# From float32r to scaled fp16 pairs in the dense stages of a recurrent kernel, with power-of-two scales found on the way

## The chip, the cores and the metric

The kernel runs on one core of a Trainium2 chip. Its engines are TensorE (PE, matrix products into PSUM), VectorE (DVE), ScalarE (ACT), GpSimd (POOL) and SyncE (SP, which issues the DMAs); each follows its own list of instructions in order and they meet through semaphores. The metric is the device time in microseconds of one execution.

## What is computed

Two layers with residuals, for 16 sequences of 512 steps with 512 features. The first is a two-layer block with a low-rank term made from a condition vector; the second is a recurrence.

```python
c = layernorm(cond) * gamma + beta
w = gelu(c @ W1 + bias1) @ W2 + bias2           # 512 x 16384, split into a1, b1, a2, b2 of 512 x 8 per sequence
u = einsum('btd,bdr->btr', x, a2)
mid = gelu(x @ base_down + einsum('btr,blr->btl', u, b2))
v = einsum('blr,btl->btr', b1, mid)
x = 2 * x + mid @ base_up.T + einsum('bkr,btr->btk', a1, v)
xW = x @ Wx + b
h[t] = tanh(xW[:, t] + h[t - 1] @ Wh)           # 512 steps, one after the other
return x + h
```

## The kernel before

**Layout.** Features lie on the partitions (KT = 4 tiles of 128), columns are 16 sequences times 32 steps, COLS = 512. The 512 steps of the recurrence are cut into 16 chunks of 32.

**The recurrence** (`chunk`, all engines). A step n has 32 products of 128x128 weights with 32 columns in fp16 (L1091: the state as a high and a low half, `hs`, times two parts of Wh) in two halves f = 0, 1 of the output features. `place` (L596, L599) on ScalarE has put x W of the step beside them in the same PSUM tile. VectorE sums the parts (L925, `z`), ScalarE takes tanh (L679, `hf`), VectorE splits the result into `hs` (L930 high, L933 low) and TensorE starts the next step. GpSimd adds h to x1 (L556), once a step; tanh of a step waits for the addition three steps back, since `hf` has four buffers.

**The dense stages.** While the recurrence works on chunk c, chunk c + 1 goes through its stages, and c + 2 through the first of them. The order is a table of slots: slot r of chunk n is run in step r of scan chunk n - 1, a negative slot in step r + 32 of scan chunk n - 2. `dense_slot(n, r)` stands in every engine's list and is called once a step behind the recurrence's part. The stages are `mid` (slots -1 to 9), `out` (11 to 21) and `xw` (21 to 29), of 48 products each, 128x128 weights with 512 columns (L1075): every operand is held as a float32r high part and its residual, and three passes are made, high x high, high x low, low x high. The rank terms add 16 products of 256 columns to `mid` and `out` (L1078), and `rank_in` (L1064) makes u in slot -2 and v in slot 10. Around them, for each of four tiles: VectorE transposes x (L830, `xt`), ScalarE rounds it to the high part (L616, `xhi`), VectorE takes the residual (L839, `xlo`); ScalarE computes gelu twice from PSUM, in full and rounded (L639, L640, slots 4, 5, 7, 9), VectorE the residual (L865, `mlo`); VectorE makes x1 (L869, slots 15, 17, 18, 21), ScalarE and VectorE split it (L645, L874); ScalarE evacuates x W (L652, `xwev`). VectorE also transposes finished output back (L888, `turn_y`). For u and v VectorE selects the diagonal blocks (L845), rounds them (L848) and takes the residual (L852); ScalarE copies the parts in place (L625, L632).

**Ahead of the recurrence** lies a load phase of `STREAM` = 40 half steps, in which W2 streams in (L476), the factors a1, b1, a2, b2 are made, the weights are split and chunk 0 goes through its dense stages. In the last chunk, where there is no dense work, TensorE gets three filler products a step (L1237, fp16, 128x128 weights with 512 columns of `wh_s`, into a PSUM bank that nobody reads).

The kernel's own order for two of the engines, in a step:

```python
for f in range(2): place(n + 1, f)              # ScalarE, behind tanh of both halves
if c + 1 < NC: dense_slot(c + 1, t)
if c + 2 < NC: dense_slot(c + 2, t - TC)
```

## Time and profile before

| what | value |
|---|---|
| median of 3 runs | 1217.7 us (1214.39 to 1218.43) |
| the profiled execution, its own time | 1219.28 us |
| its span, first to last instruction | 1217.2 us |
| mean granted TensorE clock | 0.987 of full |
| load phase, to the first step of the recurrence | some 134 us |
| a chunk of 32 steps with dense work | 67.9 us |
| the last chunk, without | some 57 us |

Busy time is the share in which an engine had an instruction under way; of TensorE it says little, since products overlap. The chain of work that ended last is the view that tells which engine sets the end. A row of the chain in order of time has its start, its length and its number of instructions; a row of the timeline has start, length, engine, line, operation, output and inputs, and in brackets how long the engine had been idle before it and who ended that.

### The profile page before, as it was taken

How to read it: one execution, taken by the hardware profiler on the slowest of the kernel's cores; microseconds unless marked ns; L12 is line 12 of the kernel's file. 1: busy time of each engine (PE TensorE's matmuls, PEld its weight loads, DVE VectorE, ACT ScalarE, POOL GpSimd, SP SyncE). 2: the span in 40 equal slices, each digit the busy share in tenths (PEclk: the TensorE clock that was granted, in tenths of full speed). 3: DMA queues.
4: the chain of work that ended last, by engine and by line, in shares of the span. 5: the costliest groups of instructions: out<-in, count | busy, mean ns of one | idle time of the engine just before them, and what ended most of it. 6: DMA issues, size and time to landing. Idle time of an engine off the chain costs nothing.

```text
span 1217.2 us, 50835 instructions
## 1 busy us (share of the span) xinstructions
PE 1189.4 (98%) x21046; PEld 959.8 (79%) x21046; DVE 893.3 (73%) x3648; ACT 640.5 (53%) x2648; POOL 254.6 (21%) x523
## 2 busy tenths in 40 slices
PE   8977999999999999999999999999999999999998
PEld 7544888888888888888888888888888888888755
DVE  4433577887877787887877777878778777877676
ACT  4121455656555655656555655656555556555443
POOL 0000122222222222222222222222222222222221
PEclk8888999999999999999999999999999999999999
DMA  9899211312221221312221221212121211102021
GB/s 316 314 397 324 36 20 21 54 21 37 36 36 23 37 38 20 55 20 41 34 37 23 38 34 29 46 20 49 26 38 31 35 29 31 27 3 37 2 46 28
DMA packets 260565, 75.73 MB, mean 62 GB/s; under 512 B 247952, under 2 KB 248096, under 8 KB 260336
## 3 DMA queue, kind: packets, MB, share of 16 engines
q1 hardware_dynamic: 258112, 72.35, 25.2%
q8 instruction: 166, 2.72, 1.1%
q14 instruction: 63, 0.52, 0.2%
q10 hardware_dynamic: 2224, 0.14, 0.2%
HBM read 55.68 MB, written 16.78 MB: 60 GB/s over the span
## 4 chain that ended last, share of the span: by engine, by line
PE 92%; DMA 4%; ACT 1%; DVE 1%; issue 1%; SPq 0%; POOLq 0%; POOL 0%
PE bulk L1075 47%; PE rec L1091 34%; PE bulk L1078 5%; DMA work<-in_L_cond_W_dram 4%; PE bulk L1064 2%; PE bulk L1053 2%; ACT rec L599 1%; DVE z L925 1%; PE rec L978 0%; PE bulk L1237 0%; PE bulk L1204 0%; SPq L486 0%; PE rec L1075 0%; PE bulk L1019 0%; ACT gel L639 0%
## 5 line engine op out<-in xcount | busy, mean ns | idle before, releaser
L1091 PEld LDWEIGHTS rec<-hs,wh_s 128*128 128x128 f16 x16352 | 443.4, 96 | 134.1 <-DVE hs L933 124.0
L1091 PE MATMUL rec<-hs,wh_s 128*128 128x32 f16 x16352 | 492.8, 177 | 6.2 <-ACT rec L599 6.2
L679 ACT ACTIVATE hf<-z 128x32 f32<-128x32 f32 x1024 | 232.6, 230 | 435.5 <-DVE z L925 399.4
L556 POOL TENSOR_TENSOR work<-work,hf 128x64 f32<-128x64 f32 x512 | 253.2, 495 | 957.8 <-DVE hs L933 956.8
L925 DVE TENSOR_REDUCE z<-rec 128x32 f32<-128x96 f32 x1022 | 262.8, 257 | 190.6 <-PE rec L1091 165.4
L1075 PE MATMUL bulk<-mid_s,up_s 128*128 128x512 f32 x768 | 222.9, 410 | 0.6 <-ACT mid_s L640 0.5
L933 DVE SCALAR_TENSOR_TENSOR hs<-hf,hs 128x32 f16<-128x32 f32 x1022 | 196.6, 192 | 35.2
L1075 PE MATMUL bulk<-act_x,down_s 128*128 128x512 f32 x768 | 219.9, 410 | 0.0
L1075 PE MATMUL bulk<-act_s,wx_s 128*128 128x512 f32 x756 | 208.4, 408 | 0.0
L930 DVE TENSOR_SCALAR hs<-hf 128x32 f16<-128x32 f32 x1022 | 181.4, 178 | 6.3 <-ACT hf L679 4.9
L599 ACT ACTIVATE rec<-work 128x32 f32<-128x32 f32 x1022 | 184.9, 213 | 0.0
L1075 PEld LDWEIGHTS bulk<-mid_s,up_s 128*128 128x128 f32 x768 | 132.6, 189 | 21.2 <-ACT mid_s L640 1.5
L1075 PEld LDWEIGHTS bulk<-act_x,down_s 128*128 128x128 f32 x768 | 132.2, 189 | 21.1 <-issue 3.3
L1075 PEld LDWEIGHTS bulk<-act_s,wx_s 128*128 128x128 f32 x756 | 132.2, 189 | 21.0 <-issue 0.6
L652 ACT ACTIVATE work<-bulk,bs,scl 128x512 f32<-128x512 f32 x62 | 48.2, 777 | 26.8 <-PE bulk L1075 26.8
L869 DVE SCALAR_TENSOR_TENSOR work<-work,bulk 128x512 f32<-128x512 f32 x64 | 43.7, 683 | 14.1 <-PE bulk L1078 14.1
L1053 PE MATMUL bulk<-work,h_rep 128*32 128x256 f32 x512 | 39.4, 432 | 14.5 <-DMA work<-in_L_cond_W_dram 12.9
L1078 PE MATMUL bulk<-rank_s,b_s 128*128 128x256 f32 x256 | 49.2, 298 | 0.0
L865 DVE TENSOR_TENSOR mid_s<-gel,mid_s 128x512 fp32r<-128x512 f32 x64 | 43.7, 684 | 4.7 <-ACT mid_s L640 4.7
L625 ACT CAST rank_s<-rank_p 32x128 fp32r<-32x128 f32 x128 | 37.4, 292 | 16.5 <-DVE rank_p L848 15.4
L874 DVE TENSOR_TENSOR act_s<-work,act_s 128x512 fp32r<-128x512 f32 x64 | 43.8, 686 | 1.1 <-ACT act_s L645 0.9
L1078 PEld LDWEIGHTS bulk<-rank_s,b_s 128*128 128x128 f32 x256 | 40.2, 192 | 5.1 <-issue 1.6
(129 smaller groups left out, 681.2 us busy)
## 6 DMA issues: line engine op xcount, KB each, us to landing
work<-in_L_cond_W_dram SPq DMA_DIRECT2D x33, 1024.0 KB, 8.1
out_dram<-work SPq DMA_DIRECT2D x240, 64.0 KB, 2.5
work<-in_x_dram SPq DMA_DIRECT2D x224, 64.0 KB, 3.9
work<-in_x_dram SPq DMA_DIRECT2D x8, 256.0 KB, 9.7
work<-in_L_cond_base_up_dram SPq DMA_DIRECT2D x1, 1024.0 KB, 8.1
work<-in_L_cond_base_down_dram SPq DMA_DIRECT2D x1, 1024.0 KB, 12.9
wh_f<-in_L_cond_Wh_dram SPq DMA_DIRECT2D x1, 1024.0 KB, 16.5
wh_f<-in_L_cond_Wx_dram SPq DMA_DIRECT2D x1, 1024.0 KB, 5.4
```

Source lines behind the costliest of these rows:

```text
L556: nc.gpsimd.tensor_tensor(to, xs, hf[:, t % 4], ALU.add).then_inc(sum_done, 1)
L599: nc.scalar.activation(R[f][:, :, PARTS, :], xw[:, c % 2].rearrange("p k (b t) -> p k b t", t=TC)[:, f * HT:(f + 1) * HT, :, t], ACT.Copy) ...
L652: nc.scalar.activation(xw[:, n % 2, m], bank(at["xw_banks"][m]), ACT.Identity, bias=bs[:, m:m + 1], scale=fwd).then_inc(xw_done, 1)
L679: nc.scalar.activation(hf[:, t % 4, half], z[:, half], ACT.Tanh, scale=inv_reg).then_inc(tanh_done, 1)
L874: nc.vector.tensor_tensor(act_s[:, LO, m], x1[n % 3][:, m], act_s[:, HI, m].bitcast(F32), ALU.subtract).then_inc(x1lo_done, 1)
L925: nc.vector.tensor_reduce(z[:, half], R[f].rearrange("p m j b -> p m b j"), AX.X, ALU.add).then_inc(z_done, 1)
L930: nc.vector.tensor_scalar(hs[:, half, 0, :], hf[:, t % 4, half], H_SCALE, None, ALU.mult).then_inc(hi_done, 1)
L933: nc.vector.scalar_tensor_tensor(out=hs[:, half, 1, :], in0=hf[:, t % 4, half], scalar=H_SCALE, in1=hs[:, half, 0, :], op0=ALU.mult, op1=A ...
L1053: last = nc.tensor.matmul(bulk[j * SQ:(j + 1) * SQ, BANK_ROW + n % 2, 0:WCOLS], h_rep[:, half * HK + k].rearrange("p g e b -> p (g e b)"), ...
L1075: mm = nc.tensor.matmul(bank(banks[m]), w_s[:, w, k, m * P:(m + 1) * P], src[:, a, k, :], start=(i in starts), stop=(i in ends), skip_grou ...
L1078: mm = nc.tensor.matmul(bank(banks[m])[:, k * GC:(k + 1) * GC], rank_f[:, -1 - p, k, m * P:(m + 1) * P], rank_s[:, k * GC:(k + 1) * GC], s ...
L1091: last = nc.tensor.matmul(R[fo][:, m, 0:PARTS, :], wh_s[:, q, k, n * P:(n + 1) * P], hs[:, k, :, :], start=(m == k == q == 0), stop=(k == ...
```

## The change

Chunks 0 to 2 keep their dense stages. From chunk `F16_FROM` = 3 on, so in the scan chunks 2 to 14:

- The operands of the three dense stages are pairs of fp16 (high part and residual) in place of float32r pairs, still three passes. The rank products (L1078) and `rank_in` stay as they are.
- fp16 has a narrow range, so each operand is scaled by a power of two. The scale follows from a bound: for x, the absolute sums of the columns of a partition (ScalarE, `accum_out`); for gelu, the bound of x, the sum of u and the largest weights; for x1, the absolute sums of gelu and v. A bound per partition becomes the largest over all partitions in this way: GpSimd writes the column times the unit matrix (`diagonal`, 128x128), TensorE multiplies it with a matrix of ones (`cross`, in steps 18, 1 and 13), VectorE reduces the result from PSUM and masks out the exponent (steps 20, 3 and 15), GpSimd forms the scales from it with one-column operations, each waiting for the one ahead.
- Gelu is computed once from PSUM, with a scale; the fp16 high part is a scaled copy of it (`ghi`, slots 5, 6, 8, 9), with the residuals a step later than before.
- x1's doubling, so far part of L869, is done by GpSimd: eight additions of 128x256 in steps 24 to 31 (`DOUBLE_AT`), since x1 is now scaled out of PSUM in the same VectorE operation.
- x is transposed a good part of a chunk earlier (steps 1, 2, 13, 14); x1 gets a fourth buffer.
- The weights are turned into scaled fp16 pairs on the way: seven maxima on VectorE (`top_of`, six in the load phase, one in step 1), exchanged between partitions by a write to HBM and a broadcast read; scales in step 14; then in steps 42 to 79 36 scaled copies on ScalarE and 24 additions and subtractions of 128x512 on GpSimd (`convert`).
- `place` writes both halves of x W in one ScalarE operation of 64 columns in every step of the kernel.

```diff
+F16_FROM = 3
+XT16_AT, XT16_FIRST = (-31, -30, -19, -18), (-21, -20, -19, -18)
+XSUM_AT, XSUM_FIRST = (-30, -29, -18, -17), (-19, -18, -17, -16)
+XTOP_AT, XSCALE_AT = -16, -12
+UTOP_AT, USCALE_AT = -1, 3
+GTOP_AT, GSCALE_AT = 11, 15
+GHI_AT, MLO_AT = (5, 6, 8, 9), (6, 7, 9, 10)
+W_SCALE_AT = 14
+CROSS_AT = (XTOP_AT + 2, UTOP_AT + 2, GTOP_AT + 2)
+DOUBLE_AT = 24
+TOPS_AT = (11, 13, 23, 12, 28, 20)
+CONVERT_AT = (F16_FROM - 2) * 32 + 10
...
+            sp.dma_start(w_tops.rearrange("(q j) -> q j", j=7), wtop[:]).then_inc(w_out, 16)
+            sp.wait_ge(w_out, 16)
+            sp.dma_start(w_all[:], w_tops.rearrange("(o n) -> o n", o=1).broadcast_to([P, P * 7])).then_inc(w_back, 16)
...
+            def diagonal(n, e, column):
+
+                i = 3 * (n - F16_FROM) + e
+                if i > 0:
+                    pool.wait_ge(crossed, i)
+                nc.gpsimd.tensor_tensor(diag[:], ident[:], spread(column, P), ALU.mult).then_inc(diag_set, 1)
...
+            def state_top(n):
+
+
+                pool.wait_ge(gsum_done, (KT + 1) * (n - F16_FROM + 1))
+                link(nc.gpsimd.tensor_tensor(gr[:, 0:2], gsum[:, 0:2], gsum[:, 2:4], ALU.add))
+                link(nc.gpsimd.tensor_tensor(gr[:, 0:1], gr[:, 0:1], gr[:, 1:2], ALU.add))
+                link(nc.gpsimd.tensor_tensor(gr[:, 0:1], gr[:, 0:1], kb[:, 1:2], ALU.mult))
+                link(nc.gpsimd.tensor_tensor(gr[:, 1:2], gsum[:, 4:5], kb[:, 3:4], ALU.mult))
+                link(nc.gpsimd.tensor_tensor(gr[:, 0:1], gr[:, 0:1], gr[:, 1:2], ALU.add))
+                link(nc.gpsimd.tensor_tensor(gr[:, 0:1], gr[:, 0:1], x_most[:, n % 2, 1:2], ALU.add))
+                diagonal(n, 2, gr[:, 0:1])
...
+                j = r - DOUBLE_AT
+                if 0 <= j < 2 * KT:
+                    if j == 0:
+                        pool.wait_ge(x1lo_done, (n + 1) * KT)
+                    part = x1[n % 4][:, j // 2, j % 2 * (COLS // 2):(j % 2 + 1) * (COLS // 2)]
+                    nc.gpsimd.tensor_tensor(part, part, part, ALU.add).then_inc(doubled, 1)
...
-                nc.scalar.activation(R[f][:, :, PARTS, :],
-                                     xw[:, c % 2].rearrange("p k (b t) -> p k b t", t=TC)[:, f * HT:(f + 1) * HT, :, t],
+                nc.scalar.activation(RX, xw[:, c % 2].rearrange("p (f m) (b t) -> p f m b t", f=2, t=TC)[:, :, :, :, t],
                                      ACT.Copy).then_inc(xw_placed, 1)
...
+                    if n >= F16_FROM:
+                        nc.scalar.activation(gel[:, m], bulk[:, at["mid_banks"][m], :], ACT.Gelu,
+                                             scale=scale_of(n, I_MID)).then_inc(gel_f, 1)
+                        continue
                     nc.scalar.activation(gel[:, m], bulk[:, at["mid_banks"][m], :], ACT.Gelu).then_inc(gel_f, 1)
                     nc.scalar.activation(mid_s[:, HI, m], bulk[:, at["mid_banks"][m], :], ACT.Gelu).then_inc(gel_done, 1)
+                for m in tile_at(at["ghi"], r):
+                    act.wait_ge(gel_f, n * KT + m + 1)
+                    act.wait_ge(uscale_done, n - F16_FROM + 1)
+                    nc.scalar.activation(g16[:, HI, m], gel[:, m], ACT.Copy, scale=scale_of(n, S_G)).then_inc(gel_done, 1)
...
+                if n >= F16_FROM and r == GSCALE_AT:
+                    dve.wait_ge(crossed, 3 * (n - F16_FROM) + 3)
+                    link(nc.vector.tensor_reduce(gr[:, 1:2], bank(BANK_U)[:, 0:P], AX.X, ALU.max))
+                    power(gr[:, 2:3], gr[:, 1:2]).then_inc(g_powered, 1)
...
+            def cross(n, e):
+
+
+                pe.wait_ge(diag_set, 3 * (n - F16_FROM) + e + 1)
+                pe.wait_ge(rank_sel, 2 * n + e)
+                if e == 0 and n > F16_FROM:
+                    pe.wait_ge(g_powered, n - F16_FROM)
+                nc.tensor.matmul(bank(BANK_U)[:, 0:P], ones[:], diag[:], start=True, stop=True,
+                                 skip_group_check=True).then_inc(crossed, 1)
...
-                    dense(out, i, at["out_banks"], up_s, mid_s, a1_s, out_mm)
+                    dense(out, i, at["out_banks"], *((up_s, mid_s) if n < F16_FROM else (up16, g16)), a1_s, out_mm)
```

Three places in the engines' lists. ScalarE, steps 9, 10 and 11 of scan chunk 6; `gel` and `mid_s` are gelu in full and rounded. Before:

```order
L679 ACTIVATE hf<-z 128x32 x2
L599 ACTIVATE rec<-work 128x2x16 x2
L639 ACTIVATE gel<-bulk 128x512
L640 ACTIVATE mid_s<-bulk 128x512
L679 ACTIVATE hf<-z 128x32 x2
L599 ACTIVATE rec<-work 128x2x16 x2
```

and of the change, where `g16_51` is the fp16 pair, `cs` holds the scales, `gsum` the absolute sums and `rank` is v:

```order
L991 ACTIVATE hf<-z 128x32 x2
L861 ACTIVATE rec<-work 128x2x2x16
L924 ACTIVATE gel<-bulk,cs 128x512
L932 ACTIVATE g16_51<-gel,cs 128x512
L991 ACTIVATE hf<-z 128x32 x2
L861 ACTIVATE rec<-work 128x2x2x16
L889 ACTIVATE g_junk,gsum<-gel 128x512
L991 ACTIVATE hf<-z 128x32 x2
L861 ACTIVATE rec<-work 128x2x2x16
L889 ACTIVATE g_junk,gsum<-gel 128x512
L894 ACTIVATE rank_p<-rank,cs 128x128
L900 ACTIVATE g_junk,gsum<-rank 128x128
```

Step 9 keeps two large operations, the second now a copy of the first one's output; steps 10 and 11, which had none, get one and three.

TensorE, steps 10 to 13, before (v, then recurrence and dense `out` in turn):

```order
L1064 MATMUL bulk<-gel,b1_f 32x128 x16
L1091 MATMUL rec<-hs,wh_s 128x32 x32
L1075 MATMUL bulk<-mid_s,up_s 128x512 x5
L1091 MATMUL rec<-hs,wh_s 128x32 x32
L1075 MATMUL bulk<-mid_s,up_s 128x512 x6
L1091 MATMUL rec<-hs,wh_s 128x32 x32
L1075 MATMUL bulk<-mid_s,up_s 128x512 x5
```

and of the change:

```order
L1441 MATMUL bulk<-gel,b1_f 32x128 x16
L1468 MATMUL rec<-hs,wh_s 128x32 x32
L1452 MATMUL bulk<-g16_51,up16_52 128x512 x5
L1468 MATMUL rec<-hs,wh_s 128x32 x32
L1452 MATMUL bulk<-g16_51,up16_52 128x512 x6
L1468 MATMUL rec<-hs,wh_s 128x32 x32
L1480 MATMUL bulk<-diag,ones 128x128
L1452 MATMUL bulk<-g16_51,up16_52 128x512 x5
```

The dense products stay in their steps; the crossing comes in ahead of the five of step 13.

GpSimd, from step 11 of a scan chunk. Before, its whole list in the recurrence is one row; the rows ahead of it set up the unit matrix and a mask:

```order
L533 AFFINE_SELECT ident<-ident 128x128
L539 AFFINE_SELECT mask_b<-mask_b 128x8
L542 AFFINE_SELECT mask_b<-mask_b 128x8
L539 AFFINE_SELECT mask_b<-mask_b 128x8
L542 AFFINE_SELECT mask_b<-mask_b 128x8
L556 TENSOR_TENSOR work<-work,hf 128x64 x512
```

and of the change, steps 20 to 26 (`xr` and `cs` are the bound of x and the scales, L809 is the addition of h, L795 the doubling of x1):

```order
L809 TENSOR_TENSOR work<-work,hf 128x64 x4
L671 TENSOR_TENSOR xr<-turn_bits,xr 128x1
L719 TENSOR_TENSOR cs<-k_inv,xr 128x2
L720 TENSOR_TENSOR x_most<-xr,kb 128x1
L721 TENSOR_SCALAR x_most<-xr 128x1
L722 TENSOR_TENSOR cs<-k_pow,xr 128x1
L809 TENSOR_TENSOR work<-work,hf 128x64 x4
L795 TENSOR_TENSOR work<-work 128x256
L809 TENSOR_TENSOR work<-work,hf 128x64
L795 TENSOR_TENSOR work<-work 128x256
```

One addition a step becomes the addition plus short lists of one-column operations, and one large operation in each of the steps 24 to 31.

## Rows read from the trace of the kernel before

**Rows 1.** The page: busy time of each engine.

```profile
PE 1189.4 (98%) x21046; PEld 959.8 (79%) x21046; DVE 893.3 (73%) x3648; ACT 640.5 (53%) x2648; POOL 254.6 (21%) x523
```

**Rows 2.** The page: chain that ended last, by engine.

```profile
PE 92%; DMA 4%; ACT 1%; DVE 1%; issue 1%; SPq 0%; POOLq 0%; POOL 0%
```

**Rows 3.** Busy us of PE, PEld, DVE, ACT, POOL, clock, DMA: scan chunk 8 and last.

```profile
681.90:749.80 67.90, 67.90 (x1271) 56.30 (x1268) 53.40 (x223) 39.08 (x164) 16.15 (x32) 1.00 0.21 34
...
1156.80:1213.90 57.10, 52.36 (x1114) 34.37 (x1110) 41.91 (x208) 22.72 (x126) 11.37 (x32) 1.00 0.18 35
```

**Rows 4.** The chain in order of time, last chunk: start, length, engine, line, count.

```profile
1173.34 0.65 PE bulk L1237 x3
```

**Rows 5.** The same view, scan chunk 8 of the kernel.

```profile
706.95 1.46 PE bulk L1075 x6
708.41 0.81 PE rec L1091 x32
709.22 1.25 PE bulk L1075 x5
...
739.38 1.48 PE bulk L1075 x6
```

**Rows 6.** The same view, load phase: ones times the weight scale.

```profile
50.73 0.32 PE bulk L1191 x2
```

**Rows 7.** The timeline, TensorE, load phase: 16 fp32 products in two passes.

```profile
9.97 3.75 PE L993 MATMUL bulk<-cT,work 128*128 128x16 f32 x32
```

**Rows 8.** The timeline, ScalarE, steps 9 and 10 of scan chunk 8.

```profile
702.10 0.60 ACT L639 ACTIVATE gel<-bulk 128x512 f32<-128x512 f32 x1 [0.47 <-PE bulk L1078]
702.60 0.59 ACT L640 ACTIVATE mid_s<-bulk 128x512 fp32r<-128x512 f32 x1
703.07 0.35 ACT L679 ACTIVATE hf<-z 128x32 f32<-128x32 f32 x2
```

**Rows 9.** Groups by line and form: busy us, mean ns, idle before.

```profile
L652 ACT ACTIVATE work<-bulk,bs,scl 128x512 f32<-128x512 f32 x62 | 48.2, 777 | 26.8 <-PE bulk L1075 26.8
...
L760 DVE TENSOR_REDUCE wmax<-wh_f 128x1 f32<-128x2048 f32 x1 | 2.3, 2278 | 0.0
```

**Rows 10.** The timeline, VectorE, behind step 11 of scan chunk 8.

```profile
705.77 0.30 DVE L845 COPY_PREDICATED rank<-mask,bulk 128x128 f32<-128x128 uint32 x1
```

**Rows 11.** The timeline, GpSimd, at the kernel's start.

```profile
1.28 0.29 POOL L533 TENSOR_SCALAR_AFFINE_SELECT ident<-ident 128x128 f32<-128x128 f32 x1 [0.23 <-POOL mask_b L531]
1.53 0.19 POOL L539 TENSOR_SCALAR_AFFINE_SELECT mask_b<-mask_b 128x8 f32<-128x8 f32 x1
1.79 0.19 POOL L542 TENSOR_SCALAR_AFFINE_SELECT mask_b<-mask_b 128x8 f32<-128x8 f32 x1
```

**Rows 12.** The timeline, all engines, scan chunk 8: two additions of h.

```profile
701.90 0.36 POOL L556 TENSOR_TENSOR work<-work,hf 128x64 f32<-128x64 f32 x1 [1.30 <-DVE hs L933]
...
703.98 0.68 DVE L865 TENSOR_TENSOR mid_s<-gel,mid_s 128x512 fp32r<-128x512 f32 x1
704.14 0.74 POOL L556 TENSOR_TENSOR work<-work,hf 128x64 f32<-128x64 f32 x1 [1.88 <-DVE hs L933]
```

**Rows 13.** The same, chunk 0, where two residuals follow each other.

```profile
180.93 0.19 DVE L933 SCALAR_TENSOR_TENSOR hs<-hf,hs 128x32 f16<-128x32 f32 x1
...
181.25 0.19 DVE L933 SCALAR_TENSOR_TENSOR hs<-hf,hs 128x32 f16<-128x32 f32 x1
181.36 1.45 DVE L874 TENSOR_TENSOR act_s<-work,act_s 128x512 fp32r<-128x512 f32 x2
181.52 0.74 POOL L556 TENSOR_TENSOR work<-work,hf 128x64 f32<-128x64 f32 x1 [1.93 <-DVE hs L933]
```

**Rows 14.** The timeline, SyncE's issues, start of the recurrence.

```profile
136.43 59.71 SPq L481 DMA_DIRECT2D work<-in_x_dram  x32
```

**Rows 15.** The timeline, all engines, one step of the last chunk.

```profile
1177.01 0.35 ACT L599 ACTIVATE rec<-work 128x32 f32<-128x32 f32 x2
...
1177.33 0.88 PEld L1091 LDWEIGHTS rec<-hs,wh_s 128*128 128x128 f16 x32 [0.63 <-DVE hs L933]
```

More of the change, by code:

```diff
@@ L556, in _ @@
                     nc.gpsimd.tensor_tensor(to, xs, hf[:, t % 4], ALU.add).then_inc(sum_done, 1)
+                    if n == W_SCALE_AT:
+                        weight_scales()
+                    for j in range(24):
+                        if n == CONVERT_AT + 3 + j // 2 * 3 + j % 2:
+                            convert(j)
+                    if c + 1 < NC:
+                        other(c + 1, t)
+                    if c + 2 < NC:
+                        other(c + 2, t - TC)
         @block.scalar
@@ L679, in chunk @@
                         nc.scalar.activation(hf[:, t % 4, half], z[:, half], ACT.Tanh, scale=inv_reg).then_inc(tanh_done, 1)
-                    for f in range(2) if n + 1 < T else ():
-                        place(n + 1, f)
+                    if n + 1 < T:
+                        place(n + 1)
                     if c + 1 < NC:
@@ L911, in _ @@
                     split_weight(1, wx_f, wx_s)
+                for j in tile_at(TOPS_AT, i):
+                    top_of(j)
                 dense_slot(0, i)
```

349 lines of the change are left out of this document (313 added, 36 removed).

## The prediction

> **What bounds the kernel now.** I read the page's busy shares first: TensorE is busy 98% of the span, VectorE 73%, ScalarE 53%, GpSimd 21% [rows 1]. A busy share of TensorE alone proves little, so next comes the chain that ended last: 92% of it is TensorE, 47% the 512-column dense products of L1075, 34% the small products of the recurrence (L1091) [rows 2]. The busy time by stretch then gives the clockwork: a chunk of 32 steps takes 67.9 us and PE is busy for all 67.9 of it, at the full clock; the last chunk, which has no dense work, takes 57.1 us [rows 3]. So with dense work a step takes 67.9 / 32 = 2.12 us and TensorE is the bound; without it a step takes 57.1 / 32 = 1.78 us and the round trip TensorE, VectorE, ScalarE, VectorE, TensorE is the bound. That is the floor: per chunk no more than 67.9 - 57 = 11 us can be won, whatever becomes of TensorE.
>
> **The dense products.** In the chain of scan chunk 8 a step is 0.81 us of recurrence (32 products) and then 1.25 us for five or 1.46 to 1.48 us for six dense products [rows 5]. The difference, 0.23 us, is one product; five are 1.15, so the first of a step costs about 0.09 more. The change turns both operands into fp16. The trace has that very form, though for filler work: L1237, 128x512 in fp16, three in 0.65 us [rows 4], 0.217 us each with nothing extra for the first. So a step with five goes from 1.25 to 1.08, one with six from 1.47 to 1.30: 0.165 us saved. It is no halving: the old products already run at nearly the speed of the new. In a chunk 25 of the 30 steps with dense work begin with such a product; three begin with a rank product and two with the new crossing, and save only 5 x 0.015 = 0.07 us. Sum: 25 x 0.165 + 5 x 0.07 = **-4.4 us a chunk**. Both are TensorE time on the path, as long as the round trip of 1.78 stays below 0.81 + 1.08 = 1.89.
>
> **What TensorE gains in work.** Three products of `ones` with the diagonal per chunk, in fp32. The nearest row is L1191, also `ones` in fp32: 0.32 us in the chain, in two passes, at three columns [rows 6]. Lower bound: the 32 passes of L993, 3.75 us for 16 products, 0.23 us each [rows 7]; upper bound 0.45, since 128 columns stream through. I take L1191's: 3 x 0.32 = **+0.95**.
>
> **What the other engines do to the round trip.** (a) Step 9. Now gelu is computed twice from PSUM, 0.60 and 0.59 us, one 0.50 us behind the other, and tanh of step 10 follows at 703.07, 0.97 after the first began [rows 8]. After the change the scaled gelu must be complete before `ghi` may read it. An operand that is a pointer adds 0.09 us (L652 with two takes 777 ns [rows 9], gelu with none 0.59 [rows 8]), so 0.68, a wake (0.08 where `hs` ends at 181.44 and L556 starts at 181.52 [rows 13]; I take 0.04), then 0.68 less the overlap of 0.1: tanh starts 1.30 after, 0.33 later than now, and the path runs through it: **+0.35**. (b) Step 13. The third bound is written by GpSimd in step 11: copy_predicated ends at 706.07 [rows 10], then two ScalarE operations to about 706.7, then six linked one-column operations on GpSimd at 0.26 us (L539 to L542, which waits for it: 1.53 to 1.79) and a diagonal of 128 columns, 0.3 to 0.5 [rows 11]. That is 708.7 to 709.0, while TensorE would come to the crossing at 709.22 in the old trace [rows 5], about 0.35 earlier in the new. TensorE, with five dense products queued behind it, waits between nothing and 0.6: **+0.25**. The other two crossings have shorter lists (two and three links) and should be in time. (c) Steps 3, 15 and 20: a reduction of the crossing from PSUM (0.26 to 0.30 us) and a linked mask (0.15) on VectorE beside a large operation of 0.68. The floor of 1.78 becomes about 2.3 against TensorE's 2.0 to 2.15: **+0.35** together, 0 to 0.9. (d) GpSimd and VectorE get in each other's way. The addition L556 takes 0.36 us alone and 0.74 when VectorE's L865, with two inputs from SBUF, is under way [rows 12]; and in the other direction a second L874 that meets a waiting L556 makes two of them last 1.45 us where 0.60 + 0.68 would do [rows 13]. GpSimd now doubles x1 in eight 128x256 operations in steps 24 to 31. From L556, 0.2 fixed and 0.16 for 64 columns, such an operation takes 0.84 us. The addition starts 0.27 after the second `hs` of a step (181.25 to 181.52 [rows 13]); 0.36 or, behind a residual, 0.74 of addition and 0.84 of doubling end 1.47 to 1.85 after it, and VectorE's first `hs` of the next step, 0.32 ahead of the second, wants the same port at 1.89 - 0.32 = 1.57. Four of the eight steps have such a residual: **+0.2**, 0 to 1.4.
>
> The Trainium skill, page SBUF — State Buffer, section Who interferes with whom, says the same lock of VectorE operations with two SBUF inputs and GpSimd operations is exclusive and blocks the loser fully; the trace agrees in both directions. Its page GPSIMD Engine Reference, section Performance versus the Vector engine, gives 4497 ns for a two-input operation of 2048 elements; by that an estimate for 256 columns is 0.74 us and for 512 columns 1.3 us, and the sum would come out some 3 us lower.
>
> What costs nothing: copying the rank parts on ScalarE instead of VectorE, four absolute sums of x and four of gelu, 0.6 us each, one or two a step: ScalarE is busy 39.1 of 67.9 us [rows 3] and has 1.3 us of a step between `place` and the next tanh. If that cover were gone (an accumulating operation twice as long), steps 8 and 11 would lose about 0.2 each. x is loaded a chunk earlier; SP issues 32 loads in the first 60 us of the recurrence [rows 14], and is idle most of the time. The x transposes move to steps 1, 2, 13 and 14, where VectorE has room.
>
> **x W in one operation.** Two that take 0.35 us together become one of 64 columns, surely shorter. In the last chunk they end at 1177.36, but TensorE's weight load starts at 1177.33 for `hs` [rows 15]. So at most 0.03 us a step where the round trip binds: -0.5 us for the last chunk, nothing elsewhere.
>
> **Sum.** -4.4 + 0.95 + 0.35 + 0.25 + 0.35 + 0.2 = -2.3 us a chunk, times the 13 scan chunks (2 to 14) that run an fp16 dense chunk: **-30**. Once: twelve weight tiles are converted in steps 42 to 79, 36 scaled copies on ScalarE and 24 GpSimd operations of 128x512, each 0.2 + 512 x 0.0025 = 1.5 us. Such a one ends 0.27 + 0.36 + 1.5 = 2.1 us after the previous `hs` or later, past the moment (1.57 to 1.8) the next wants the port, and a step of chunk 1 has some 0.3 us of slack; with 0.25 us a piece, **+6** (bounds 2 and 25). Seven maxima of the weights on VectorE, 2.28 us for 2048 columns [rows 9]: six lie in the load phase, where waits of 3 to 6 us for DMA stand between VectorE's operations, +1; the seventh and the reduction over 896 columns (1 us and three links) lie in chunk 0, +1.5. The maxima travel out to HBM and back behind the loads of chunk 2, the first half of the 32 from 136.43 on, which half a microsecond apiece would bring to about 145 to 150 us [rows 14]; they are wanted at step 14, about 134 + 14 x 2.2 = 165 us, so that wait is covered. Total: -30 + 6 + 2.5 - 0.5 = -22; I take **-24**, since (b), (c) and (d) are counted as if nothing of them fell into steps of six products, which have 0.33 us of slack. The profiled execution took 1219.3 us, 1217.2 of it span, and is 1.6 above the median of the three runs; 1219.3 - 24 = 1195.3, and on the runs' scale **1194 us**.
>
> **Rivals.** *All of TensorE's gain arrives* (10%): ScalarE and VectorE delays vanish in the steps' slack; -4.4 + 0.95 = -3.45 x 13 = -45, with +4 once: 1177. For it speaks that a five-product step keeps 0.12 us above the floor; against it step 10, which already shows ScalarE's delay. *Little arrives* (16%): the diagonal is late at all three crossings and the reductions count in full, 1.2 to 2 us a chunk more: 1206 to 1220. *Slower: GpSimd's large operations hold the port* (13%). The trace has one size of this addition; if its 0.36 us grew with the columns, 256 would cost 1.43 and 512 2.9 us. Then each of steps 24 to 31 finds `hs` blocked for some 0.5 us, 4 us a chunk, 50 in all, and the conversion, 2 x 2.9 + 3 x 0.5 = 7.3 us in three steps of 6.2, falls behind, +25: about 1260. It decides from 1.1 us for 128x256, where eight delays of 0.3 eat the 2.3 of a chunk. Against it: operations on GpSimd of 8 and 128 columns take 0.19 and 0.29 us [rows 11], far from proportional. *The change is not doing what it says* is excluded: the fp16 operands stand in the new order.
>
> **Chances.** Forecast 61%, for 1183 to 1206. A measurement of this kernel tells 0.3% (3.7 us) from no change, so faster means below 1214: 0.61 + 0.10 + 10 of the 16 = 0.81; same 0.06; slower 0.13. The range of 8 in 10: 1176, the first rival, up to 1218, which leaves out most of the third.
>
> **What would show it.** Chunks of 65.5 us in place of 67.9; five dense products in 1.08 us; a chunk 1 and 2 longer than the rest by 2 to 4 us; step 10 at 2.3 us; a last chunk of 56.5 to 57. Wrong if the 128x256 operation is over 1.1 us, if TensorE waits over 0.6 us for `diag`, or if the first fp16 product of a step still costs 0.09 more: then 25 x 13 x 0.09 = 29 us are gone, and with them the gain.

## The result, and the profile after

| | before | changed |
|---|---|---|
| median, us | 1217.8 (4 runs, 1214.4 to 1218.4) | 1184.2 (4 runs, 1181.1 to 1190.6) |
| ratio | 1 | 0.9736 (0.9687 to 0.9786) |
| profiled execution, us (span) | 1219.3 (1217.2) | 1190.6 (1188.9) |
| first reduction of the recurrence at | 135.7 | 137.1 |
| from there to the end | 1081.5 | 1051.8 |

The change makes the kernel 2.6% faster, 34 us by the medians. A second comparison of the same two kernels gave 1185.5 (5 runs) against 1217.6 (9 runs), 0.9732 (0.9707 to 0.9757). The profiled execution of the changed kernel is the slowest of its four. What scatters is mainly the load phase: over the twelve traces of the changed kernel and its relatives below, the first reduction lies between 127.8 and 137.1 us. Behind that point two traces of the changed kernel agree within 0.5 us (1051.8 and 1052.4). So differences are read from the first reduction (step 1) on, where the change gains 29.7 us; the remaining 2 to 4 us of the medians lie in the load phase or in its scatter.

The page of the changed kernel, busy time of each engine and then the chain that ended last by engine (before in [rows 1] and [rows 2]):

```profile
PE 1148.0 (97%) x21124; PEld 833.9 (70%) x21124; DVE 923.1 (78%) x3710; ACT 713.9 (60%) x2459; POOL 422.1 (36%) x992
...
PE 79%; ACT 6%; DVE 5%; DMA 4%; issue 3%; POOL 2%; SPq 0%; ACTq 0%; POOLq 0%
```

TensorE is still the bound, but the chain now leaves it for 21% of the span, through ScalarE and GpSimd, which [rows 2] hardly had. Busy time by stretch, of the changed kernel: scan chunks 1, 2, 8 and the last (columns as in [rows 3]):

```profile
209.24:280.40 71.16, 68.98 (x1272) 56.35 (x1269) 57.72 (x223) 51.18 (x162) 32.46 (x54) 1.00 0.20 32
280.40:350.10 69.70, 66.26 (x1276) 46.22 (x1273) 56.30 (x226) 51.93 (x170) 40.01 (x77) 1.00 0.20 33
673.98:738.72 64.74, 64.42 (x1277) 46.52 (x1274) 54.33 (x226) 43.91 (x156) 26.65 (x66) 1.00 0.22 35
1126.90:1183.80 56.90, 51.08 (x1108) 33.84 (x1105) 41.19 (x205) 19.47 (x93) 11.47 (x32) 1.00 0.18 35
```

Before, chunks 1, 2 and 8 took 67.9 each and the last 55.4, from the first reduction of its first step to that of its last (the 57.1 of [rows 3] went some steps further). Per stretch, changed minus before: chunk 0 +1.4, chunk 1 +3.3, chunk 2 +1.8, chunks 3 to 13 -3.15 each (-34.6), chunk 14 -3.1, last chunk +1.5. That sums to -29.7.

**What a chunk gained.** In chunk 8 I took every product's start up to the next product's start and summed by line. It shows where TensorE's time went, its waits included:

| TensorE, us of chunk 8 | before | changed |
|---|---|---|
| dense products, 144 | 35.51 | 29.78 |
| rank products, 32 passes | 4.06 | 5.43 |
| recurrence, 1024 | 26.31 | 26.35 |
| rank_in, 64 passes | 2.03 | 2.33 |
| crossings, 6 passes | - | 0.85 |
| sum | 67.90 | 64.75 |

Dense and rank products belong together: a rank product behind an fp16 product starts after 0.03 us and then takes longer itself, so the border between the lines moved by about 1.3 us. Together they gained 4.36 us. Inside the recurrence 0.32 was gained (most groups of 32 products take 0.80 where they took 0.81) and lost again in waits. The waits are at two places. The first, the timeline of the changed kernel in steps 9 and 10 of chunk 8 (beside [rows 8]):

```profile
693.25 0.69 ACT L924 ACTIVATE gel<-bulk,cs 128x512 f32<-128x512 f32 x1 [0.43 <-PE bulk L1455]
...
693.97 0.72 ACT L932 ACTIVATE g<-gel,cs 128x512 f16<-128x512 f32 x1
693.99 0.81 PEld L1441 LDWEIGHTS bulk<-gel,b_f 128*32 128x32 f32 x32
...
694.60 0.33 ACT L991 ACTIVATE hf<-z 128x32 f32<-128x32 f32 x2
...
695.30 0.98 PE L1468 MATMUL rec<-hs,wh_s 128*128 128x32 f16 x32 [0.24 <-DVE hs L1310]
```

Gelu starts at 693.25 and tanh at 694.60, 1.35 later; before it was 0.97. TensorE waits 0.3 us behind the rank_in products, and 0.13 around them, more than before. The second, GpSimd's list for the third bound and the crossing of step 13:

```profile
698.17 0.19 ACT L900 ACTIVATION_READ_ACCUMULATOR g_junk<-rank 128x1 f32 x1
...
698.43 0.19 POOL L743 TENSOR_TENSOR gr<-gsum 128x2 f32<-128x2 f32 x1 [0.58 <-ACT g_junk L900]
698.70 0.19 POOL L744 TENSOR_TENSOR gr<-gr 128x1 f32<-128x1 f32 x1
...
700.05 0.40 POOL L702 TENSOR_TENSOR diag<-ident,gr 128x128 f32<-128x128 f32 x1
...
700.50 0.30 PEld L1480 LDWEIGHTS bulk<-diag,ones 128*128 128x128 f32 x2 [0.18 <-POOL diag L702]
700.50 0.49 PE L1480 MATMUL bulk<-diag,ones 128*128 128x128 f32 x2
```

Six links of 0.27 us follow the sum of v, then the diagonal; TensorE has been ready since about 700.27. Everywhere else in the chunk its products start back to back, but for 0.08 us ahead of the products that make u, which the kernel before had too: steps 3, 15 and 20, with reduction and mask, have no wait, and the doubling in steps 24 to 31 brings none. Reduction and mask of step 15, on VectorE:

```profile
705.67 0.28 DVE L1177 TENSOR_REDUCE gr<-bulk 128x1 f32<-128x128 f32 x1
705.99 0.21 DVE L1144 TENSOR_TENSOR gr<-gr,expo 128x1 uint32<-128x1 uint32 x1
```

Lengths of some steps (from one step's first reduction to the next's), chunk 8, and of chunks 1 and 2 where they were longest:

| step | before | changed |
|---|---|---|
| 2 (five products) | 2.06 | 1.88 |
| 1 (five, crossing) | 2.04 | 2.19 |
| 10 | 1.97 | 2.39 |
| 13 | 2.06 | 2.44 |
| 46, chunk 1 | 2.04 | 3.02 |
| 52, chunk 1 | 2.06 | 3.82 |
| 67, chunk 2 | 2.17 | 3.19 |
| 77, chunk 2 | 2.06 | 3.31 |
| last chunk, most steps | 1.77 | 1.82 |

### The profile page after: what moved, and what is told of

It is laid out like the page before. It is cut to its first block, busy times and chain, and to the rows that moved or that the text cites. A ratio compares the mean times of both kernels' runs of the same rounds, so it can differ in the third digit from the quotient of the medians.

```text
span 1188.9 us, 51698 instructions
## 1 busy us (share of the span) xinstructions
PE 1148.0 (97%) x21124; PEld 833.9 (70%) x21124; DVE 923.1 (78%) x3710; ACT 713.9 (60%) x2459; POOL 422.1 (36%) x992
## 4 chain that ended last, share of the span: by engine, by line
PE 79%; ACT 6%; DVE 5%; DMA 4%; issue 3%; POOL 2%; SPq 0%; ACTq 0%; POOLq 0%
PE bulk L1452 38%; PE rec L1468 30%; PE bulk L1455 5%; DMA work<-in_L_cond_W_dram 4%; PE bulk L1430 2%; PE bulk L1441 1%; DVE z L1302 1%; DVE hs L1307 1%; PE bulk L1480 1%; ACT rec L861 1%; ACT hf L991 1%; DVE hs L1310 1%; DVE g L1221 1%; ACT g_junk L889 1%; ACT gel L924 1%
## 5 line engine op out<-in xcount | busy, mean ns | idle before, releaser
L809 POOL TENSOR_TENSOR work<-work,hf 128x64 f32<-128x64 f32 x384 | 200.0, 521 | 570.4 <-DVE hs L1310 570.3
L1307 DVE TENSOR_SCALAR hs<-hf 128x32 f16<-128x32 f32 x1022 | 191.7, 188 | 25.1 <-ACT hf L991 15.5
L1452 PE MATMUL bulk<-g,up 128*128 128x512 f16 x624 | 162.6, 379 | 0.0
L1452 PE MATMUL bulk<-x,down 128*128 128x512 f16 x624 | 160.3, 379 | 0.0
L1452 PE MATMUL bulk<-h,wx 128*128 128x512 f16 x624 | 153.6, 378 | 0.0
L861 ACT ACTIVATE rec<-work 128x64 f32<-128x64 f32 x511 | 136.0, 266 | 0.0
L809 POOL TENSOR_TENSOR x_d<-x_d,hf 128x64 f32<-128x64 f32 x96 | 50.3, 524 | 105.0 <-DVE hs L1310 105.0
L1452 PEld LDWEIGHTS bulk<-h,wx 128*128 128x128 f16 x624 | 51.7, 96 | 46.9
L1452 PEld LDWEIGHTS bulk<-g,up 128*128 128x128 f16 x624 | 51.7, 97 | 41.8
L1452 PEld LDWEIGHTS bulk<-x,down 128*128 128x128 f16 x624 | 50.7, 97 | 40.3
L1455 PE MATMUL bulk<-rank_s,a_s 128*128 128x256 f32 x256 | 50.2, 318 | 0.0
L795 POOL TENSOR_TENSOR work<-work 128x256 f32<-128x256 f32 x72 | 43.9, 610 | 0.0
```

The source lines that it names most:

```text
L795: nc.gpsimd.tensor_tensor(part, part, part, ALU.add).then_inc(doubled, 1)
L809: nc.gpsimd.tensor_tensor(to, xs, hf[:, t % 4], ALU.add).then_inc(sum_done, 1)
L861: nc.scalar.activation(RX, xw[:, c % 2].rearrange("p (f m) (b t) -> p f m b t", f=2, t=TC)[:, :, :, :, t], ACT.Copy).then_inc(xw_placed, 1)
L1307: nc.vector.tensor_scalar(hs[:, half, 0, :], hf[:, t % 4, half], H_SCALE, None, ALU.mult).then_inc(hi_done, 1)
L1452: mm = nc.tensor.matmul(bank(banks[m]), w_s[:, w, k, m * P:(m + 1) * P], src[:, a, k, :], start=(i in starts), stop=(i in ends), skip_grou ...
L1455: mm = nc.tensor.matmul(bank(banks[m])[:, k * GC:(k + 1) * GC], rank_f[:, -1 - p, k, m * P:(m + 1) * P], rank_s[:, k * GC:(k + 1) * GC], s ...
```

## The experiments

Each kernel is the changed one but for its edit, unless said otherwise. "Rest" is the time from the first reduction to the end; 1051.8 for the changed kernel. But for the last two kernels, each ran once, so its effect is read from its trace, step by step, and not from its total.

**x W placed in two operations.**

```diff
-                        place(n + 1)
+                        for f in range(2):
+                            place(n + 1, f)
...
-                        pe.wait_ge(xw_placed, n)
+                        pe.wait_ge(xw_placed, 2 * (n - 1) + 1)
                         quadrant(0, 0)
+                        pe.wait_ge(xw_placed, 2 * (n - 1) + 2)
```

> The changed kernel with x W of a step placed by two ScalarE operations of 32 columns again, TensorE waiting for the first ahead of its first eight products and for the second later. Theory A (TensorE needs only the first half to start: the first of two ends 0.21 us after its start, the single one 0.26): a step of the last chunk goes from 1.82 back to 1.77 us, the last chunk loses 1.5 us, no other step changes. Rival B (the longer step of the last chunk comes from something else in the change): it stays at 1.82.

The last chunk, by stretch, and one of its steps (the first products start 0.14 us behind the end of the first small operation, as in [rows 15]; in the changed kernel, second fence, 0.14 behind the end of the single one):

```profile
1126.00:1181.46 55.46, 51.09 (x1108) 33.84 (x1105) 41.03 (x204) 22.26 (x124) 11.52 (x32) 1.00 0.18 35
...
1144.59 0.35 ACT L861 ACTIVATE rec<-work 128x32 f32<-128x32 f32 x2
...
1144.94 0.23 PE L1470 MATMUL rec<-hs,wh_s 128*128 128x32 f16 x3 [0.16 <-ACT rec L861]
```

```profile
1145.96 0.26 ACT L861 ACTIVATE rec<-work 128x64 f32<-128x64 f32 x1
...
1146.36 0.95 PE L1468 MATMUL rec<-hs,wh_s 128*128 128x32 f16 x32 [0.21 <-ACT rec L861]
```

The last chunk is back at 55.5 and its step at 1.77. TensorE needs only half of x W for its first products: of two operations of 0.21 us the first counts, and a single one takes 0.26. The same edit alone, in the kernel before:

> The kernel before with nothing changed but x W placed by one operation of 64 columns. Theory A: its last chunk (31 steps from the first reduction to the last) grows from 55.4 to 56.9 us, a step from 1.77 to 1.82; chunks of 67.9 us stay. Rival B: no change, 1.77.

```profile
678.53:746.43 67.90, 67.90 (x1271) 56.30 (x1268) 53.46 (x222) 36.21 (x132) 16.10 (x32) 1.00 0.21 34
1153.52:1210.81 57.29, 51.86 (x1108) 34.11 (x1105) 41.26 (x205) 19.50 (x93) 11.01 (x31) 0.97 0.17 35
```

Steps of 1.82 again, 67.9 where TensorE is the bound. 57.3 in place of 56.9 comes almost wholly from the second step in the stretch (2.13); TensorE's granted clock sank there, 0.97 over the stretch in the row. The theory stands for the last chunk: there this part of the change costs 1.5 us. But "no other step changes" did not hold. With two operations in the changed kernel, chunks 0, 1 and 2 are longer by 0.2, 0.15 and 0.3 us, so its rest is 1050.6, only 1.2 less; in the kernel before, chunk 0 is 0.2 shorter with the single operation. Why those steps prefer the single one was not tried.

**The third bound begun early.** Four of the six links need only gelu's sums and x's bound:

```diff
-                pool.wait_ge(gsum_done, (KT + 1) * (n - F16_FROM + 1))
+                pool.wait_ge(gsum_done, (KT + 1) * (n - F16_FROM) + KT)
...
+                link(nc.gpsimd.tensor_tensor(gr[:, 0:1], gr[:, 0:1], x_most[:, n % 2, 1:2], ALU.add))
+                pool.wait_ge(gsum_done, (KT + 1) * (n - F16_FROM + 1))
                 link(nc.gpsimd.tensor_tensor(gr[:, 1:2], gsum[:, 4:5], kb[:, 3:4], ALU.mult))
                 link(nc.gpsimd.tensor_tensor(gr[:, 0:1], gr[:, 0:1], gr[:, 1:2], ALU.add))
-                link(nc.gpsimd.tensor_tensor(gr[:, 0:1], gr[:, 0:1], x_most[:, n % 2, 1:2], ALU.add))
```

> The changed kernel, with GpSimd's list for the third bound begun once the four sums of gelu are there; only two of its six one-column operations are left to follow the sum of v. Theory A (TensorE waits 0.23 us in step 13 for this list): step 13 falls from 2.44 to 2.21, 0.23 us in each of 13 chunks, 3 us. Rival B (the step is long for the crossing itself): 2.44 stays.

```profile
672.43:736.93 64.50, 64.26 (x1277) 46.45 (x1274) 54.34 (x226) 43.94 (x156) 26.73 (x66) 1.00 0.21 36
```

Step 13 is 0.25 shorter (2.19), the chunk too, rest 1048.8. The wait was this list.

**The last gelu copy behind tanh.**

```diff
-GHI_AT, MLO_AT = (5, 6, 8, 9), (6, 7, 9, 10)
+GHI_AT, MLO_AT = (5, 6, 8, 10), (6, 7, 9, 10)
```

In step 10 the copy is issued ahead of gelu's sum, and the dense products of `out` wait for each residual where they first read that tile.

> The changed kernel, with the scaled copy of the fourth gelu tile on ScalarE behind tanh and x W of step 10 in place of ahead of them; the dense products of step 11 wait for each residual where they first read that tile, not for all four. Theory A (the copy ahead of tanh is what TensorE waits for at step 10, 0.3 us at the rank products and 0.15 at the next): step 10 falls from 2.39 to about 2.1, step 11 takes some of it back since the residual now ends later on VectorE (1.92 to 2.05): 0.2 to 0.4 us a chunk, 3 to 5 us in all. Rival B (the gelu itself, not the copy, is late): steps 10 and 11 keep their sum of 4.31.

```profile
690.09 0.69 ACT L928 ACTIVATE gel<-bulk,cs 128x512 f32<-128x512 f32 x1 [0.44 <-PE bulk L1459]
...
690.89 0.53 ACT L995 ACTIVATE hf<-z 128x32 f32<-128x32 f32 x2
...
691.53 0.71 ACT L889 ACTIVATE g<-gel,cs 128x512 f16<-128x512 f32 x1
...
692.27 0.75 DVE L1225 SCALAR_TENSOR_TENSOR g<-gel,cs,g 128x512 f16<-128x512 f32 x1 [0.40 <-ACT g L889]
...
697.46 0.49 PE L1484 MATMUL bulk<-diag,ones 128*128 128x128 f32 x2 [0.43 <-POOL diag L702]
```

Tanh starts 0.80 us behind the start of gelu instead of 1.35. The waits behind the rank_in products and in the recurrence of the next step are gone (these two groups take 1.01 and 0.81 us, where they took 1.32 and 0.98); 0.22 of it comes back as a wait for the residual in the next dense products, and steps 10 and 11 together lose 0.24 us. So the copy was what they waited for. Yet the chunk is 64.87, 0.1 longer: the sums stand behind the copy now, the third bound is later by as much, and step 13 grows by 0.35. The gain moved into the wait that the experiment ahead of this one removes. My expectation named the copy's effect and missed who is queued behind it.

**What the scaling costs.** Bounds and scales for chunks 3 and 4 alone, waits for them capped:

```diff
+BOUND_TO = F16_FROM + 2
...
-                if n >= F16_FROM and r in CROSS_AT:
+                if F16_FROM <= n < BOUND_TO and r in CROSS_AT:
```

> The changed kernel, in which the bounds and scales are found for chunks 3 and 4 alone; all later chunks take the scales of these (so the guard against overflow is left out): no absolute sums on ScalarE, no crossings, no reductions and masks, no lists on GpSimd in 11 of the 13 chunks. It measures what the scaling costs. Theory A (on TensorE's path lie the crossings, 0.31 + 0.33 + 0.22 us, and the 0.23 us wait for the third diagonal, nothing else): a chunk goes from 64.75 to 63.7, 12 us in all; steps 1, 13 and 18 shrink, step 10 stays at 2.39. Rival B (the sums on ScalarE and the reductions on VectorE cost too): 63.2 or less, and steps 3, 10, 15 or 20 shrink as well.

```profile
661.57:725.24 63.67, 63.43 (x1271) 45.59 (x1268) 53.46 (x221) 38.61 (x135) 21.45 (x41) 1.00 0.22 36
```

63.7, as theory A has it: 1.07 us a chunk, of which 0.85 are the crossings (0.30 + 0.33 + 0.22) and 0.21 the wait for the third diagonal; rest 1041.0. ScalarE has 5.3 and VectorE 0.9 us less to do, which brings nothing. Steps 3, 15 and 20 do shrink, by 0.20, 0.19 and 0.38, as B wants; but 4, 16 and 21 grow by 0.16, 0.16 and 0.30. A step measured between VectorE's reductions shows when VectorE came, and with the mask it comes some 0.2 to 0.3 later; TensorE has slack for that, and its products stay back to back.

**The doubling in pieces of 128x512**, once where an addition of 0.80 us stands ahead, once where it takes 0.36:

```diff
-                if 0 <= j < 2 * KT:
+                for k in tile_at((24, 25, 27, 29), r):
...
-                    part = x1[n % 4][:, j // 2, j % 2 * (COLS // 2):(j % 2 + 1) * (COLS // 2)]
+                    part = x1[n % 4][:, k]
```

> The changed kernel with x1 doubled in four GpSimd operations of 128x512 in place of eight of 128x256, in steps 24, 25, 27 and 29, where a two-input VectorE operation makes the addition of h ahead of it last 0.80 us. An estimate from the conversion (128x512 takes 1.16 us): such an operation ends 0.08 + 0.80 + 1.16 = 2.04 us after the last hs, the next hs asks 1.56 us after it in a step of five products and 1.78 in one of six. Theory A (the shared port blocks VectorE, and it costs only beyond the slack of the step, 0.06 and 0.28): step 25 grows from 1.88 to 2.3, steps 24, 27 and 29 by 0 to 0.1; 0.4 to 0.7 us a chunk, 5 to 9 us. Rival B (the port isn't what delays hs): nothing changes. Rival C (a lock of any length costs its full time): 0.3 to 0.5 in all four steps, 20 us.

> The same four operations of 128x512, in steps 26, 28, 30 and 31, where the addition of h takes 0.36 us. They end 0.08 + 0.36 + 1.16 = 1.60 us after the last hs. Theory A: no step changes by more than 0.05, nothing in the total. Rival C: each of the four steps grows.

 

One piece and the `hs` that it meets in the first; then chunk 8 of the first; then of the second kernel (slots 26, 28, 30, 31):

```profile
729.41 1.04 POOL L795 TENSOR_TENSOR work<-work 128x512 f32<-128x512 f32 x1
...
729.96 0.54 DVE L1307 TENSOR_SCALAR hs<-hf 128x32 f16<-128x32 f32 x1
...
678.48:744.21 65.73, 65.09 (x1277) 46.39 (x1274) 55.70 (x227) 43.86 (x156) 26.12 (x61) 1.00 0.21 35
```

```profile
667.26:732.13 64.87, 64.53 (x1277) 46.49 (x1274) 54.67 (x227) 43.85 (x155) 26.20 (x62) 1.00 0.22 35
```

`hs`, 0.18 us alone, lasts 0.54 and ends 0.04 to 0.05 behind GpSimd's operation. The chunk grows by 1.0 us, rest 1064.0. It is the mechanism of theory A and more than its size: the growth is in steps 25, 26, 28 and 30 (0.33, 0.24, 0.21, 0.19). An operation of step 25 delays the `hs` of step 26, so the slack that counts is the next step's, and I had set slacks a step too early. In the other steps the very same operations cost 0.1 a chunk: what decides is whether the operation is over when `hs` asks, not how long it is. The 0.1 is all in step 0, behind the operation of step 31 (1.97 for 1.88), a little more than the 0.05 that theory A allowed. Behind the other three the steps kept their lengths, though the `hs` behind step 28's operation lasted 0.31 us, so a short delay is absorbed. Rival C is out.

**The conversion**, GpSimd's part cut to one column, then 24 of ScalarE's 36 copies:

```diff
-                    nc.gpsimd.tensor_tensor(w_s[:, HI, k], w_s[:, HI, k].bitcast(F32), w16[:, HI, k],
+                    nc.gpsimd.tensor_tensor(w_s[:, HI, k, 0:1], w_s[:, HI, k, 0:1].bitcast(F32), w16[:, HI, k, 0:1],
```

> The changed kernel with the 24 GpSimd operations of the conversion cut from 512 columns to 1 (the low fp16 weight is then the scaled old low part alone, without the rounding rest of the high part); ScalarE does its 36 scaled copies as before. Scan chunks 1 and 2 now take 71.2 and 69.7 us where 67.9 and 64.8 would be without a conversion: 8.2 us. Theory A (GpSimd holds the port against hs and the bound's mask, steps 52, 67 and 77): more than half of it goes, 3 to 4 us stay, and steps 52, 67 and 77 fall to 2.2 to 2.4. Rival B (ScalarE's queue, three large operations in step 46): at least 6 us stay.

> The changed kernel with 24 of ScalarE's 36 scaled copies of the conversion cut to 1 column, written to a scratch tile (the low fp16 weights are then made from unscaled parts); the 24 GpSimd operations of 128x512 stay. Theory A (the port): 4 to 5 of the 8.2 us stay, steps 52, 67 and 77 long as before. Rival B (ScalarE's queue): at most 2 us stay, step 46 falls from 3.02 to 2.1.

Chunks 1 and 2 without GpSimd's part:

```profile
207.93:277.37 69.44, 68.49 (x1273) 56.25 (x1270) 53.30 (x224) 51.18 (x163) 20.16 (x54) 1.00 0.20 33
277.37:344.97 67.60, 65.57 (x1277) 46.10 (x1274) 53.41 (x226) 51.74 (x171) 27.82 (x76) 1.00 0.21 34
```

Of 8.2 us 4.3 stay, so GpSimd's operations cost 3.9, slightly under the "more than half" of theory A. Steps 52, 67 and 77 fall to 2.20, 2.15 and 2.39. The timeline of the changed kernel shows how, in step 52, with a mask of one column that lasts 1.25 us and ends with GpSimd's operation, and in step 77, where `hs` does:

```profile
255.11 1.29 POOL L771 TENSOR_TENSOR down<-down_s 128x512 f16<-128x512 f32 x1
255.17 1.25 DVE L1144 TENSOR_TENSOR xr<-xr,expo 128x1 uint32<-128x1 uint32 x1
...
311.48 1.27 POOL L771 TENSOR_TENSOR wx<-wx_s 128x512 f16<-128x512 f32 x1
...
311.69 1.11 DVE L1307 TENSOR_SCALAR hs<-hf 128x32 f16<-128x32 f32 x1 [0.56 <-ACT hf L991]
```

Without two thirds of ScalarE's copies chunks 1 and 2 take 70.9 and 69.0: 7.2 us stay, more than the 4 to 5 of A, with steps 52, 67 and 77 at 3.80, 3.18 and 3.10. B's sign fails: step 46 keeps 3.0 us in both kernels (3.02 and 2.97). Its ScalarE queue, without GpSimd's part: four rank copies, a sum, a weight copy of the third that had stayed, and tanh last:

```profile
236.24 1.22 ACT L916 CAST rank_s<-rank_p 32x128 fp32r<-32x128 f32 x4
...
237.48 0.63 ACT L885 ACTIVATE x_junk<-x_d 128x512 f16<-128x512 f32 x1
238.02 0.19 ACT L885 ACTIVATION_READ_ACCUMULATOR x_junk<-x_d 128x1 f32 x1
238.11 0.71 ACT L965 ACTIVATE down<-down_s,sw 128x512 f16<-128x512 f32 x1
238.72 0.33 ACT L991 ACTIVATE hf<-z 128x32 f32<-128x32 f32 x2
...
238.97 0.18 DVE L1307 TENSOR_SCALAR hs<-hf 128x32 f16<-128x32 f32 x1 [1.20 <-ACT hf L991]
```

So it is ScalarE's queue that makes this step long, as B has it, and my cut missed the copy that stands there. Cut one at a time, GpSimd's part gives back 3.9 and the 24 copies 1.0 us. How the other 3.3 divide between the 12 copies that stayed, the first fp16 chunk's sums and what the two parts cost only together was not tried.

**All together.** Two placing operations, the early bound, the late copy, and the conversion by two lists of steps:

```diff
+COPY_SLOTS = [n for n in range(42, 84) if n not in (44, 45, 64, 65, 76, 77)]
+SUM_SLOTS = (45, 47, 49, 50, 53, 56, 58, 60, 62, 64, 65, 66, 68, 69, 71, 72, 74, 76, 77, 78, 80, 81, 83, 84)
```

> The changed kernel with four things put together: x W placed in two operations, the third bound's list on GpSimd begun early, the fourth scaled gelu copy behind tanh of step 10, and the conversion moved: no scaled copy on ScalarE in the steps in which it copies rank parts, and no 128x512 operation on GpSimd in steps 52, 67 and 79, where VectorE has a mask. The late copy alone moved its gain into step 13; with the list begun early that step should be free. Theory A: chunks of 64.3 us or less (64.75 - 0.25 - 0.2), last chunk 55.5, scan chunks 1 and 2 together 3 us shorter than the 140.9 of the changed kernel; from the first reduction to the end 1051.8 - 13 x 0.45 - 1.4 - 3 = 1041.5 us. Rival B (the late copy makes the bound late again, or the conversion only moves its delays): 1046.

```profile
200.20:269.56 69.36, 68.84 (x1273) 56.22 (x1270) 54.95 (x223) 52.73 (x192) 28.83 (x50) 1.00 0.20 33
269.56:341.53 71.97, 67.41 (x1277) 45.67 (x1274) 61.16 (x226) 56.17 (x205) 43.45 (x80) 1.00 0.19 32
663.15:727.49 64.34, 64.19 (x1277) 46.42 (x1274) 54.38 (x227) 46.44 (x188) 26.24 (x66) 1.00 0.22 36
```

Chunk 8 is at 64.3 and the last at 55.5, as expected; late copy and early bound together give 0.4 a chunk, where the copy alone gave -0.1. Chunk 1 gains 1.8, but chunk 2 loses 2.3, 1.79 of it in step 84, into which I had put a 128x512 operation beside the mask. Rest 1045.7, so B for the conversion. The last attempt takes that operation away:

```diff
+COPY_SLOTS = sorted([n for n in range(42, 83) if n not in (44, 45, 64, 65, 76, 77)] + [80])
+SUM_SLOTS = (45, 47, 49, 50, 53, 56, 58, 60, 62, 64, 65, 66, 68, 69, 71, 72, 74, 76, 77, 78, 80, 81, 82, 83)
```

> As the combined kernel, but with the last copies and additions of the conversion a step earlier (two copies in step 80), so that no 128x512 operation on GpSimd stands in step 84, where VectorE masks the bound of x: there the combined kernel lost 1.79 us. Theory A (only the neighbour in step 84 mattered): step 84 back to 2.3 to 2.7, scan chunk 2 at 70 to 70.5, chunks 1 and 2 together 139.5 to 140; from the first reduction to the end about 1043; a median some 8 us below the changed kernel's of the same comparison. Rival B (the delay only moves to step 83): chunk 2 stays at 72.

```profile
277.25:348.59 71.34, 67.37 (x1277) 45.66 (x1274) 60.40 (x227) 56.14 (x205) 43.53 (x80) 1.00 0.20 32
670.17:734.48 64.31, 64.17 (x1277) 46.40 (x1274) 54.35 (x226) 46.40 (x188) 26.25 (x66) 1.00 0.22 36
```

> The changed kernel once more, in the same comparison as the final one and in more rounds. Theory A (its step lengths are fixed, and what scatters between executions is the load phase alone): from the first reduction to the end 1051.8 us as in its first trace, whatever the total; the median within 3 us of 1184. Rival B (the steps scatter too): the two traces differ by more than 1 us behind the first reduction.

In one comparison: the final kernel 1179.6 us (0.9696 of before, 0.9673 to 0.9719), the changed one 1185.5 (0.9732, 0.9707 to 0.9757), before 1217.6. The two intervals overlap a little, so the 6 us between the medians are not settled by them; the two traces show it: rest 1045.4 against 1052.4, 7 us less, of it 4.9 in chunks 3 to 13, 0.5 in chunk 14 and 1.5 in the last. Step 84 kept 0.82 of its delay and chunk 2 stayed at 71.3, near rival B. The trace shows why: the operation of step 83 is still under way when the `hs` of step 84 asks, the same reach into the next step as with the doubling.

```profile
324.13 1.27 POOL L773 TENSOR_TENSOR wx<-wx_s 128x512 f16<-128x512 f32 x1
...
324.42 1.01 DVE L1314 TENSOR_SCALAR hs<-hf 128x32 f16<-128x32 f32 x1
```

Moving the conversion gained 1.8 in chunk 1 and lost 1.6 in chunk 2. Since chunk 2 also holds the 0.4 of the other edits, the new lists of the conversion were worth nothing in sum; a kernel with the old lists and the other three edits was not run. The changed kernel's second trace has the step lengths of its first, within 0.04 us, but for two at the border to the last chunk (2.09 and 2.10 for 1.82), so theory A of it holds.

## Why the prediction was right, and where it wasn't

1194 us was forecast, 1176 to 1218; it is 1184.2. Direction and main mechanism were right, the size fell short by 10 us on the medians. The terms summed to -22, and -24 was taken. In the recurrence, without the 1 us given to the load phase, the terms make -23, and measured are -29.7.

- **Dense products, -4.4 a chunk: right**, -4.36. A product goes from 0.231 to 0.216 us, and the first of a step has none of the 0.09 that the old form had there. The warning sign at the end of the prediction did not come.
- **Crossings, +0.95: near**, 0.85 (0.30, 0.33, 0.22). The two-pass row of [rows 6], at three columns, was the right neighbour: 128 columns brought nothing that shows in 0.30 to 0.33 us. At the end of a step, behind other products, one costs 0.22.
- **(a) step 9 and 10, +0.35: right**, 0.43, and the experiment showed the copy ahead of tanh to be the cause. Step 10 was to be 2.3 and is 2.39. The gelu with a pointer takes 0.68 as worked out from [rows 9], the copy 0.72 instead of 0.68.
- **(b) wait for the diagonal, +0.25: right**, 0.23, shown by starting the list earlier.
- **(c) reductions and masks, +0.35: wrong, 0.** The two operations are there, with 0.25 to 0.28 and about 0.2 us. The step that failed is the "floor of 1.78 becomes about 2.3": it adds them to the round trip in full, but VectorE's large operation of the step stands behind `hs` and has until the next reduction, and what is late there (0.2 to 0.3) is taken up by the next step. Removing them moved no product of TensorE's.
- **(d) the port, +0.2: mechanism right, size wrong, 0.** The doubling takes 0.61 us, not 0.84. My fit used "0.2 fixed and 0.16 for 64 columns" of the addition, whose time holds more than its columns. The estimate made from the Trainium skill, page GPSIMD Engine Reference, section Performance versus the Vector engine, 0.74, was nearer; the row has 0.61:

```profile
L795 POOL TENSOR_TENSOR work<-work 128x256 f32<-128x256 f32 x72 | 43.9, 610 | 0.0
```

- **Not foreseen: -0.32 a chunk in the recurrence.** Its groups of 32 take 0.80 us behind fp16 products and took 0.81 behind the old ones (behind a rank product, which is float32r in both, 0.81 in both). Why was not tried. Terms: -4.36 + 0.85 + 0.43 + 0.23 - 0.32 = -3.17, against -2.3 forecast. Of the 0.85 by which the forecast was short, 0.55 are (c) and (d), 0.3 this; times 13 chunks, 11 us.
- **Conversion, +6: near**, 8.2, inside its bounds. But the cause was only half of it: the forecast names the port alone (3.9 us), and what a 0.71 us copy does to ScalarE's queue in a step with rank copies and a sum was not in it.
- **Chunk 0, +1.5: near**, +1.4. It sits in the step ahead of the scales (4.50 us for 2.52; steps 14 and 15 give 0.55 back), where the reduction over 896 columns took 1.83 us, not the 1 us forecast. The load phase's +1 can't be told within 9 us of scatter. The reduction's row:

```profile
166.78 1.83 DVE L1291 TENSOR_REDUCE wall<-w_all 128x7 f32<-128x896 f32 x1
```

- **Placing x W in one operation, -0.5: wrong, +1.5 in the last chunk.** The failed step: "in the last chunk they end at 1177.36, but TensorE's weight load starts at 1177.33 for `hs`". I took the end of both operations as what TensorE waits for. The code waits for the first (`xw_placed, 2 * (n - 1) + 1`) ahead of its first products, and that first one ended at 1177.22. The pair's shorter sum was of no use; the diff showed the second wait going.
- **Range and rivals.** "All of TensorE's gain arrives" was nearer to what came than its 10%: the steps' slack did take up VectorE's delays, though not ScalarE's and GpSimd's. The port did not make the kernel slower because each operation is over before `hs` asks. The point from which that decides was put at 1.1 us; four operations of 1.04 us behind an addition of 0.80 cost 1.0 us a chunk, and the same four behind one of 0.36 next to nothing. So the limit is a moment in the step, with the addition in it, and not a length. One sum among the rivals was off: 1.2 to 2 us a chunk more are 16 to 26 us, so the second rival's range begins at 1210, not 1206.

What holds the range up is that the gain was counted per product and per step from rows, and the extra work placed on a clock of the step. That 1184.2 still lies inside 1183 to 1206 is in part luck: the 11 us of the chunks were offset by 4 us that conversion and placing cost beyond their forecast, and without these it would have been 1180. In the 13 chunks the errors of (c) and (d) went the same way: work added to an engine that isn't the bound was charged in full.
